# GpSimd scales each context matrix by sixteen tensor_scalar operations of 128 columns in place of one tensor_tensor of 2048

## What is computed

```
def _L0_xattn_ref(x, weight):                  # weight = the context
    xq = quant_dequant_act_1x128(x)            # per row and block of 128 columns
    wq = quant_dequant_weight_128x128(weight)  # per block of 128 x 128
    return jnp.einsum('emk,enk->emn', xq, wq)
...
x = x + jnp.tanh(g_xattn[0]) * _L0_xattn_ref(_layernorm(x, axis=-1), ctx_2048)
x = x + jnp.tanh(g_ffn[0]) * _L0_ffn_ref(_layernorm(x, axis=-1), ...)   # top 2 of 8 experts, capacity 640
```

## Time and profile before

| | |
|---|---|
| median of 3 runs | 884.56 us (884.31 to 886.72) |
| the profiled execution | 886.47 us |
| its span, first to last instruction | 884.8 us |
| busy share: PE, DVE, ACT, POOL | 92%, 68%, 41%, 27% |
| mean granted TensorE clock | 0.972 |
| shares of the chain that ended last: PE, DVE, ACT, POOL | 81%, 9%, 3%, 1% |

### The profile page before, as it was taken

The page is one execution under the profiler, slowest core; times in us unless marked ns, Lnnn a source line. Parts: engine busy times, 40 slices in busy tenths (PEclk is TensorE's granted clock), DMA queues, the critical chain, the costliest instruction groups (busy, mean ns, idle before and its releaser), DMA issues.

```text
span 884.8 us, 12004 instructions
## 1 busy us (share of the span) xinstructions
PE 812.7 (92%) x4249; PEld 387.7 (44%) x4250; DVE 605.1 (68%) x958; ACT 366.1 (41%) x586; POOL 235.2 (27%) x208
## 2 busy tenths in 40 slices
PE   0289998779999999999999999999999999999996
PEld 0134657434434444444444444444444444444442
DVE  5999778767485777678678567856785677565430
ACT  4798968534223441444043404340434143414310
POOL 2231341866343023303320322023202320232010
PEclk9999996599999999999999999999999999999998
DMA  8600725575295329425852564257435743422000
GB/s 306 266 0 1 286 95 191 184 187 97 73 218 197 120 88 278 143 95 141 260 154 95 122 234 153 96 105 251 143 107 99 258 131 118 100 55 72 1 25 24
DMA packets 79257, 123.16 MB, mean 139 GB/s; under 512 B 43358, under 2 KB 43374, under 8 KB 75136
## 3 DMA queue, kind: packets, MB, share of 16 engines
q1 hardware_dynamic: 68032, 93.33, 34.0%
q0 software_dynamic: 10912, 29.50, 12.1%
q10 hardware_dynamic: 288, 0.00, 0.0%
HBM read 96.52 MB, written 18.95 MB: 131 GB/s over the span
## 4 chain that ended last, share of the span: by engine, by line
PE 81%; DVE 9%; ACT 3%; DMA 2%; issue 2%; POOL 1%; another core or an unknown queue 1%; POOLq 0%; DVEq 0%; ACTq 0%
PE mm L824 37%; PE mm L754 36%; PE mm L541 2%; PE mm L794 2%; DVE region L1229 2%; DVE region L1225 2%; ACT region L882 1%; PE mm L733 1%; DMA region<-in_x 1%; PE mm L569 1%; DVE region L1199 1%; PE xT_ps L569 1%; DMA region<-x_split,row_next 1%; DMA lists<-notes,goals 1%
## 5 line engine op out<-in xcount | busy, mean ns | idle before, releaser
L824 PE MATMUL mm<-region,w_split 128*128 128x512 f16 x1536 | 335.6, 381 | 6.4 <-DVE region L1531 3.7
L754 PE MATMUL mm<-region 128*128 128x512 f16 x1536 | 337.3, 380 | 0.0
L824 PEld LDWEIGHTS mm<-region,w_split 128*128 128x128 f16 x1536 | 150.6, 98 | 190.1 <-issue 7.0
L754 PEld LDWEIGHTS mm<-region 128*128 128x128 f16 x1536 | 149.2, 98 | 183.3 <-issue 5.8
L1108 ACT ACTIVATE region<-mm 128x512 f16<-128x512 f32 x128 | 76.4, 597 | 319.5 <-PE mm L824 308.0
L1531 DVE SCALAR_TENSOR_TENSOR region<-mm,region 128x512 f16<-128x512 f32 x128 | 88.5, 691 | 108.5 <-ACT region L1108 100.0
L467 POOL DMA_INDIRECT out<-region,back_now x40 | 63.9, 1598 | 174.0 <-DVE region L1544 143.4
L1534 DVE SCALAR_TENSOR_TENSOR region<-w_stage,w_scale,region 128x512 f16<-128x512 f32 x128 | 96.1, 751 | 0.0
L1111 ACT ACTIVATE region<-w_stage,w_scale 128x512 f16<-128x512 f32 x128 | 91.2, 713 | 0.0
L1316 DVE TENSOR_REDUCE top<-w_stage 128x1 f32<-128x512 f32 x112 | 75.9, 678 | 1.6 <-DMA w_stage<-in_L_ffn_w 1.6
L1327 DVE SCALAR_TENSOR_TENSOR w_split<-w_stage,w_scale,w_split 128x2048 f16<-128x2048 f32 x32 | 73.7, 2348 | 1.7 <-DVE region L1560 1.7
(11 more groups left out here) (187 smaller groups left out, 569.7 us busy)
## 6 DMA issues: line engine op xcount, KB each, us to landing
w_stage<-in_L_ffn_w SPq DMA_DIRECT2D x64, 1024.0 KB, 5.3
region<-in_x SPq DMA_DIRECT2D x4, 1024.0 KB, 13.1
x_split<-region SPq DMA_DIRECT2D x8, 512.0 KB, 3.0
out<-region SPq DMA_DIRECT2D x4, 1024.0 KB, 6.4
w_stage<-in_ctx SPq DMA_DIRECT2D x2, 1024.0 KB, 11.4
region<-in_ctx SPq DMA_DIRECT2D x2, 1024.0 KB, 14.9
region<-x_split,row_next POOLq DMA_INDIRECT x40, 7.2
region<-out,row_next POOLq DMA_INDIRECT x40
```

The costliest lines, as they stand in the source:

```text
L754: mm = pe.matmul(mm2[s % 2][:, :], hidden[:, hh, f, s * P:(s + 1) * P], w2_split[:, wh, f, :], start=(f == 0 and hh + wh == 0), stop=(f == ...
L824: mm = pe.matmul(products(f), w1_split[:, wh, k, f * P:(f + 1) * P], xT[:, xh * KD + k, 0:WIDE], start=(k == 0 and wh + xh == 0), stop=(k ...
```

## The change

`by_blocks` on POOL is rewritten. In place of one product of two tensors (the context, and the 16 scales spread over 128 columns each) it issues sixteen operations, one for each block of 128 columns, each with one scale per partition. Only the last of the sixteen raises the semaphore, and only the first waits. The seven calls keep their places.

```
             def by_blocks(b, scales):
-                parts = ctx[b].rearrange("p (j n) -> p j n", n=P)
-                return nc.gpsimd.tensor_tensor(parts, parts, scales.unsqueeze(2).broadcast_to([P, JC, P]), ALU.mult)
+                for j in range(JC):
+                    block = ctx[b][:, j * P:(j + 1) * P]
+                    last = nc.gpsimd.tensor_scalar(block, block, scales[:, j:j + 1], None, ALU.mult)
+                return last
```

## The result

The changed kernel took 917.04 us (median of 4 runs, 915.12 to 918.40), the kernel before 884.97 (4 runs, 884.31 to 886.72): a ratio of 1.0361, interval 1.0342 to 1.0380, or 32.1 us more. The profiled execution took 915.12 us, its span is 913.4 (884.8 before), its mean granted clock 0.962 (0.972 before). The prediction was 889.0 with a range up to 901: the direction was right, the size far off. Ratios and intervals leave out executions in a slower state of the chip; the medians of the experiments run over all executions, which moves none of them by more than 0.4 us.

What follows compares the result with a forecast made beforehand. PE bounds the kernel from 168 us on, so only the expert loop's start can move. 2.4 + 2.8 - 0.5 - 0.3 = 4.4 us on 884.6 gives 889.0; range 883 to 901.

Steps and rivals of the forecast that it cites:

- What one of the sixteen costs: Each 128-column piece on POOL: 0.25 us start to start, from an affine_select row; 4.0 us a context, 0.4 more than 3.61.
- (c): Rival: pieces last 0.29 to 0.40 us, the scale being a second read; at 0.36 15.6 us late, 900; chance 0.26.
- (b): Rival: port not released between back-to-back POOL operations, DVE waits for all sixteen; 885.8, or 888.8 at 0.31 a piece; chance 0.25.
- goes to the engine that has been waiting: SBUF port shared by DVE and POOL: it changes hands at an instruction's end, to whichever engine has been waiting.
- (a): Rival: pieces last 0.14 to 0.22 us; at 0.14 a gain, 882.4 to 883.2, at 0.20 gain and interleaving cancel; chance 0.19.
- (1): `context_up(1)` on POOL: ends 0.4 us later, and ACT and then DVE's L1225 with it, to 45.9.
- (2): `context_down(0)`: last piece waits 1.22 us for DVE, end near 47.3 for 45.74; `attend(0)` 1.5 late, 0.9 arrives at DVE.
- (3): `context_down(1)`: two or three pieces wait for one each of DVE's six operations; end 70.6, `attend(1, [1])` 4.6 us late.
- (4): PE's waits behind `attend(1, [1])`, 1.09, 0.50 and 0.63 us: 2.2 taken up, 2.4 left to reach `context_down(3)`.
- (5): `context_down(3)`: 0.4 longer plus two DVE operations let in, 2.8 us in all; of DVE's gain only 0.51 and 0.26 count.
- Calls costed at nothing: `context_up(2)`, `context_down(2)`, `context_up(3)`: nobody seen waiting for them, hidden by ACT's and PE's work; without that cover 0.4 us each.
- The clock: PE clock falling in the longer waits, possibly costing more than the waits; named as what could make the argument wrong, unpriced.

## Why the prediction was wrong, point by point

**The step that failed is "What one of the sixteen costs".** It took 0.25 us from the affine_select of the same block; measured are 0.58 in the kernel and 0.579 by itself. With it each undisturbed call costs 5.7 us more, not 0.4. The row was of another operation: same partitions and columns, other work for each column. Nor was the all-reduce at 0.36 an upper end. It bounds the start-up of an operation of one column, while the price here grows with the columns at 2.6 ns each, and no row of the trace before had that slope; the nearest, the product's own 1.76 ns, already made 128 columns 0.23 us without any start-up. With a start-up on top, such a product measured 0.357, in rival (c)'s span.

**"Long pieces" (c) was the right rival with too low a ceiling.** At 0.36 it gave 15.6 us. The products at 0.357 measured 19.0, and their gather was 17.5 late. The mechanism it named, the whole string of six met by `context_down(1)`, is the row of 16.54 us. The reason that it gave for long pieces, the scale as a second read, is the smaller part: 0.085 of the 0.33 us by which a piece was longer than the 0.25 taken.

**The port changes hands between pieces, rival (b) fell; but the turns are not fair ones.** DVE gets in between two of POOL's pieces, and the pair near 112 us went from 2.93 and 4.97 us to 1.20 and 1.27 in the changed kernel, and to 1.36 and 1.94 with four products of 512 columns. That the port "goes to the engine that has been waiting" does not hold for POOL: three pieces saw five of DVE's boundaries, and the six operations of the string took 9.55 us where they had taken 9.47, though four pieces of 0.58 us stood between them. Why DVE loses so little is open. **"Short pieces" (a)** fell with the 0.58. The place from which pieces stop hurting was put at 0.20; at 0.235 the loss in the prologue was down to 1.8.

**The places were right, their sizes not.** (1) `context_up(1)`: 0.4 forecast; ACT waits for it until 45.1 in place of 35.6, 9.5 later; the string it met, `round_context(0)`, was not in the prediction. (2) `context_down(0)`: 1.5 forecast at PE, 7.5 when alone (53.4 for 45.9). (3) `context_down(1)`: `attend(1, [1])` 4.6 forecast, 25.4 measured (91.44 for 66.09). (4) The slack of 2.2 us on PE was there behind a late `attend(1, [1])`, but more than half of it was lost again: with `context_down(1)` alone `attend(1, [1])` begins 13.3 us late and lasts 6.63 in place of 5.37, so its end is 14.6 late, and `attend(3, [0])` 12.3, the first gather 11.0. With `context_down(0)` alone hardly any slack was taken up: 7.5 late at `attend(0)`, 7.1 at `attend(3, [0])`. (5) `context_down(3)`: 2.8 forecast, 7.6 when alone; that DVE's gain is worth next to nothing held.

**Calls costed at nothing were not free.** `context_up(2)` was named as hidden, at 0.4 if the cover is gone. At 13 us it runs into `context_down(1)`, its neighbour on POOL's own queue. The prediction had asked who waits for it, and not what stands behind it. `context_up(3)` too lies on the chain, its third stretch (113.12), with `low_rows(0)` right behind it.

**The clock.** The prediction named it as what could make it wrong, without a price. These are windows in the changed kernel, of the wait before `attend(1, [1])` with its first matmuls, and of the wait before `attend(3, [0])` with its first matmuls (us, busy time of PE, PEld, DVE, ACT, POOL, granted clock, DMA share, GB/s):

```profile
76.40:96.90 20.50, 5.46 (x7) 2.39 (x8) 8.56 (x6) 6.72 (x17) 20.50 (x24) 0.50 0.00 0
141.20:151.50 10.30, 5.82 (x7) 2.52 (x8) 0.00 (x0) 1.61 (x5) 8.41 (x9) 0.50 0.10 36
```

and these in the kernel before, the only two at this level ahead of 138 us:

```profile
67.10:70.50 3.40, 3.40 (x6) 1.32 (x5) 3.37 (x3) 3.40 (x6) 0.00 (x0) 0.50 0.00 0
111.40:114.80 3.40, 3.14 (x14) 2.63 (x13) 3.37 (x6) 3.07 (x4) 2.70 (x1) 0.50 0.00 0
```

In the first two PE had waited long (18.3 and 7.4 us), and the granted clock is 0.50, the lower of its two levels (1.2 of 2.4 GHz). The next matmuls begin at it, about 0.83 us each (5.82 for seven) in place of 0.44 (7.03 for sixteen), and `attend(3, [0])` and `[1]` last 9.98 us in place of 7.42. That is 2.5 us on top of the wait. The same matmuls lasted 7.03 when only `context_down(1)` was in pieces and PE had no wait there; with four products they last 9.90 behind a wait of 3.2 us. A wait right ahead of them isn't the whole condition: with only `context_down(0)` in pieces they last 9.41 behind one of 0.83, and at `attend(1, [1])` the same wait of 2.53 us is followed by 5.37 us in the kernel before and by 3.67 where only `context_down(3)` was in pieces. Over the stretch ahead of the gathers the clock is a small part of the 33 us: PE is busy at the lower level for 11.3 us in place of 6.5, and if half of such time is lost, that is 2.4 us more, an estimate from the four windows. Both kernels have another stretch of some 34 us at the lower level around the beginning of the work on the experts.

**The loop lasted nearly what it lasted.** From the first gather on it is 4.4 us shorter in the one profiled execution, 0.9 by the medians (32.1 for 33.0), and from 299.50 us on equal within 0.5.

## What to carry to other kernels

Before an operation on GpSimd is replaced by "simpler" ones, measure the new form by itself at two widths: here the tensor_scalar cost 2.6 ns a column and 0.25 us of start-up, the product 1.7 ns, and a row of another operation of the same shape said nothing about it. Where another engine waits for GpSimd's result, as PE does here, and DVE has a string of two-input operations at that time, leave the operation on GpSimd whole: each piece inside the string waits for one DVE operation or two, and the loss grows fast once the call reaches into the string. Look also at the next call on the same queue, and don't add up the effects of places that delay the same point.

## What the runs showed of the hardware

- A tensor_scalar on GpSimd (f32, 128 partitions) is slower for each column than a product of two tensors: 2.6 against 2.1 ns, 1.7 with one operand spread, 0.9 for a copy. Reading the scale from SBUF adds 0.085 us to each instruction, a constant none.
- The port changes hands between back-to-back instructions of one engine too, but not evenly: six DVE operations kept their pace beside GpSimd's pieces of 0.58 us (9.55 us for the six), and the four pieces that met them lost 7.2 us.
- After waits of 3 to 9 us PE's next matmuls ran in part at half the clock: sixteen of 512 columns took 8.58 to 10.18 us, where they took 7.42 in the kernel before and 7.03 at the full clock. After shorter waits it went either way: 9.41 us behind 0.83, 7.11 behind 1.43.
